# Scores of the first attention as one float32r product over stacked high and low parts

## The reference

```
Bx  = einsum('bni,bri->bnr', x, B[adapter_ids])          # rank 16
c   = einsum('bnr,bor->bno', Bx, A[adapter_ids])         # 8 samples x 128 x 512
qkv = einsum('sbh,ph->sbp', c, weight_qkv)               # 8 groups of 4 query heads, one key, one value head
attention runs over the 8 samples s, t (causal, t <= s), separately for each of the 128 rows
x   = x + (softmax(q k^T / sqrt(128)) v) @ weight_proj^T
```

## Time and profile before

| | us |
|---|---|
| median of 3 runs | 1568.53 |
| lowest and highest | 1563.63, 1569.09 |
| the profiled execution | 1554.2 |
| its span | 1552.5 |
| PE busy | 1509.9 (97%) |
| DVE busy | 1180.2 (76%) |
| ACT busy | 893.2 (58%) |
| POOL busy | 879.2 (57%) |

### The profile page before, as it was taken

How to read it: one execution, slowest core, us unless ns; L and a number is a source line. 1 busy time by engine, 2 the same in 40 slices (tenths; PEclk the granted TensorE clock), 3 DMA queues, 4 the chain that set the end, 5 groups by cost and what they waited for, 6 DMA issues and landing times.

```text
span 1552.5 us, 27376 instructions
## 1 busy us (share of the span) xinstructions
PE 1509.9 (97%) x8984; PEld 1293.2 (83%) x8984; DVE 1180.2 (76%) x2668; ACT 893.2 (58%) x2308; POOL 879.2 (57%) x1231
## 2 busy tenths in 40 slices
PE   6899999989999999999999999999999999999997
PEld 4788888778888888888888888888888888888885
DVE  3666665767888888888888878888887888777865
ACT  2433333356666666666666666666666666666641
POOL 1111234236667666766676676667666766676521
PEclk8999999999999999999999999999999999999999
DMA  6654555322222222222222222222222222311102
GB/s 209 209 161 134 148 165 162 77 82 70 69 71 73 69 71 61 76 70 70 64 72 71 71 66 70 70 71 72 70 72 66 70 69 65 89 59 48 42 27 82
DMA packets 74085, 133.39 MB, mean 86 GB/s; under 512 B 17426, under 2 KB 27026, under 8 KB 73946
## 3 DMA queue, kind: packets, MB, share of 16 engines
q1 hardware_dynamic: 56482, 97.56, 21.2%
q0 software_dynamic: 16464, 33.85, 7.5%
q10 hardware_dynamic: 1000, 0.23, 0.1%
HBM read 107.47 MB, written 7.34 MB: 74 GB/s over the span
## 4 chain that ended last, share of the span: by engine, by line
PE 91%; DVE 3%; ACT 2%; issue 2%; POOL 1%; DMA 1%; ACTq 0%; POOLq 0%; DVEq 0%; SPq 0%
PE ps_t L948 15%; PE ps_o L739 11%; PE ps_o L741 10%; PE ps_o L740 10%; PE ps_b L739 5%; PE ps_b L741 5%; PE ps_b L740 5%; PE ps_q L741 4%; PE ps_q L740 4%; PE ps_q L739 4%; PE ps_t L762 3%; PE ps_a L739 3%; PE ps_a L793 3%; PE ps_a L741 3%; PE ps_a L740 3%
## 5 line engine op out<-in xcount | busy, mean ns | idle before, releaser
L1443 ACT ACTIVATE sm<-sm,mn 128x640 f32<-128x640 f32 x256 | 211.4, 826 | 234.5 <-DVE mn L1912 234.5
L1788 DVE TENSOR_TENSOR pT_lo<-ps_t,pT_hi 128x512 fp32r<-128x512 f32 x320 | 220.2, 688 | 113.5 <-ACT pT_hi L1366 113.3
L622 POOL DMA_INDIRECT kraw<-in_L_cond_k_cache_dram,idx_a x200 | 197.5, 988 | 89.1 <-issue 74.3
L1366 ACT ACTIVATE pT_hi<-ps_t 128x512 fp32r<-128x512 f32 x320 | 188.5, 589 | 84.7 <-PE ps_t L948 84.7
L622 POOL DMA_INDIRECT vraw<-in_L_cond_v_cache_dram,idx_a x200 | 198.7, 994 | 59.6 <-issue 59.3
L948 PE MATMUL ps_t<-ident,sm 128*128 128x128 f32 x1280 | 195.7, 275 | 3.2 <-ACT sm L1453 1.5
L948 PEld LDWEIGHTS ps_t<-ident,sm 128*128 128x128 f32 x1280 | 147.9, 140 | 51.4 <-DVE qT_lo L1788 17.9
L639 POOL TENSOR_TENSOR z<-pairs_p,zl 128x128 f32<-128x128 f32 x160 | 57.9, 402 | 206.8 <-DVE pairs_p L1652 206.8
L739 PE MATMUL ps_o<-pT_lo,v_hi 128*128 128x512 f32 x320 | 129.8, 406 | 0.0
L741 PE MATMUL ps_o<-pT_hi,v_hi 128*128 128x512 f32 x320 | 125.5, 392 | 0.0
L740 PE MATMUL ps_o<-pT_hi,v_lo 128*128 128x512 f32 x320 | 124.9, 390 | 0.0
(11 more groups left out here) (257 smaller groups left out, 4370.1 us busy)
## 6 DMA issues: line engine op xcount, KB each, us to landing
fv<-st SPq DMA_DIRECT2D x128, 128.0 KB, 2.3
tab<-tab_scratch SPq DMA_DIRECT2D x64, 256.0 KB
wraw<-n_L_attn_weight_qkv_dram SPq DMA_DIRECT2D x8, 1536.0 KB, 7.3
wpraw<-_L_attn_weight_proj_dram SPq DMA_DIRECT2D x8, 1024.0 KB, 9.4
mask<-mask_scratch SPq DMA_DIRECT2D x64, 128.0 KB
wtile<-in_L_cond_Wq_dram SPq DMA_DIRECT2D x28, 256.0 KB
wtile<-in_L_cond_Wo_dram SPq DMA_DIRECT2D x28, 256.0 KB
kraw<-in_L_cond_k_cache_dram,idx_a POOLq DMA_INDIRECT x200, 2.6
```

Source lines behind the costliest of these rows:

```text
L622: pool.indirect_dma_start(raw[:, par, c, :], None, rows_d, bass.IndirectOffsetOnAxis(idx[:, k:k + 1].bitcast(U32), 0)).then_inc(arrived[pa ...
L1366: act.activation(dst, src, ACT.Copy).then_inc(t_hi, 1)
L1443: act.activation(sm[:, h, :], sm[:, h, :], ACT.Exp, bias=mn[:, h:h + 1], scale=-1.0, accum_out=den[:, h:h + 1]).then_inc(e_done, 1)
L1788: dve.tensor_tensor(lo, src, hi.bitcast(F32), ALU.subtract).then_inc(t_lo, 1)
```

## The change

For scores_s, the high and low parts are put side by side along the contraction instead of being three products. `zlT[:, 2p:2p+2, :]` is nonzero only in the 32 rows of quarter p (two samples of 16 ranks). So three quarters' rows of one product are enough for the three terms:

- `zl3`: for the pair of samples p, the high part stands in the rows of quarter p and again in quarter p + 1, the low part in quarter p + 2 (all modulo 4). `zl_rows` (ACT, 8 copies) and `zl_low` (DVE, 4 subtractions) fill it, once.
- `mix3`: four tiles, one for each pair p, of 4 heads by 32 (p + 1) columns. Quarter p holds the high part of `mix`, quarter p + 1 the low part, quarter p + 2 the high part again. In each group `mix_copy` (ACT) makes 4 copies of 32 rows by 128, 256, 384 and 512 columns, `mix_second` (ACT) 4 copies of the same sizes, and `mix_low` (DVE) 4 subtractions of the same sizes. `mix_low` waits for all four of `mix_copy`.
- `scores_s` is one float32r product of the same width on these. Product 0 waits for the first `mix_second` and `mix_low`, product 1 for all four `mix_low`.
- POOL clears `mix3` (1280 columns) and `zl3` (1024 columns) ahead of `halfs` and `mask`.
- `wT` has three slots instead of six; `zlT` lies elsewhere.
- PE does `mix_product` ahead of `z_out(1)` (in group 0: ahead of `p_group(1)`).

```diff
-        mix = at("mix", [P, HG, P], F32, 52)
-        wT = at("wT", [P, 6, NC_, P], F32, 136)
-        zlT = at("zlT", [P, N, P], F32, 168)
+        wT = at("wT", [P, 3, NC_, P], F32, 136)
+        mix3 = at("mix3", [P, 10 * P], F32R, 142)
+        zl3 = at("zl3", [P, N, P], F32R, 168)
+        zlT = at("zlT", [P, N, P], F32, 56)
...
+        def mix_tile(p):
+            first = P * (p * (p + 1) // 2)
+            return mix3[:, first:first + P * (p + 1)].rearrange("q (h m) -> q h m", h=HG)
+        def rows(q):
+            return slice(32 * (q % 4), 32 * (q % 4) + 32)
...
+            pool.memset(mix3[:].bitcast(F32), 0.0).then_inc(zl3_ok, 1)
+            pool.memset(zl3[:].bitcast(F32), 0.0).then_inc(zl3_ok, 1)
             pool.memset(halfs[:], -0.5).then_inc(iota_ok, 1)
...
             def scores_s(g, s):
+                if s % 2 == 0:
+                    pe.wait_ge(mix_two, 4 * g + s // 2 + 1)
+                    pe.wait_ge(mix_lo, 4 * g + s // 2 + 1)
+                if s == 1:
+                    pe.wait_ge(mix_lo, 4 * g + 4)
                 if s <= 1:
-                    pe.wait_ge(mix_done, g + 1)
...
-                pe.matmul(o.rearrange("p (h m) -> p h m", h=HG), zlT[:, s, :], mix[:, :, 0:R * (s + 1)],
+                pe.matmul(o.rearrange("p (h m) -> p h m", h=HG), zl3[:, s, :], mix_tile(s // 2)[:, :, 0:R * (s + 1)],
...
             def mix_copy(g):
                 act.wait_ge(mix_full, g + 1)
-                act.activation(mix[:, :, :].rearrange("p h m -> p (h m)"), s_bank(9 * g)[:, :], ACT.Copy
-                               ).then_inc(mix_done, 1)
+                if g == 0:
+                    act.wait_ge(zl3_ok, 2)
+                src = s_bank(9 * g)[:, :].rearrange("q (h m) -> q h m", h=HG)
+                for p in range(4):
+                    act.activation(mix_tile(p)[rows(p), :, :], src[rows(p), :, 0:32 * (p + 1)], ACT.Copy
+                                   ).then_inc(mix_hi, 1)
+            def mix_second(g):
+                for p in range(4):
+                    act.wait_ge(mix_hi, 4 * g + p + 1)
+                    act.activation(mix_tile(p)[rows(p + 2), :, :], mix_tile(p)[rows(p), :, :].bitcast(F32), ACT.Copy
+                                   ).then_inc(mix_two, 1)
+            def zl_rows():
+                act.wait_ge(zT_done, 2)
+                act.wait_ge(zl3_ok, 2)
+                for p in range(4):
+                    act.activation(zl3[rows(p), 2 * p:2 * p + 2, :], zlT[rows(p), 2 * p:2 * p + 2, :], ACT.Copy
+                                   ).then_inc(zl3_hi, 1)
+                for p in range(4):
+                    act.activation(zl3[rows(p + 1), 2 * p:2 * p + 2, :], zlT[rows(p), 2 * p:2 * p + 2, :], ACT.Copy
+                                   ).then_inc(zl3_two, 1)
...
+            def mix_low(g):
+                dve.wait_ge(mix_hi, 4 * g + 4)
+                src = s_bank(9 * g)[:, :].rearrange("q (h m) -> q h m", h=HG)
+                for p in range(4):
+                    dve.tensor_tensor(mix_tile(p)[rows(p + 1), :, :], src[rows(p), :, 0:32 * (p + 1)],
+                                      mix_tile(p)[rows(p), :, :].bitcast(F32), ALU.subtract).then_inc(mix_lo, 1)
```

More of the change, by code:

```diff
@@ L1317, in _ @@
                 w_copy(0, t)
+            zl_rows()
             fold_copy(0)
             p_copy(0, 0)
+            mix_copy(0)
             p_copy(0, 1)
-            mix_copy(0)
+            mix_second(0)
             p_copy(0, 2)
@@ L1336, in _ @@
                 mix_copy(i)
+                mix_second(i)
                 p_copy(i, 1)
@@ L1627, in sums_s, with zl_low @@
                                   AX.X, ALU.add).then_inc(y_red, 1)
+            def mix_low(g):
[4 more added lines that the diff above has]
+                                      mix_tile(p)[rows(p), :, :].bitcast(F32), ALU.subtract).then_inc(mix_lo, 1)
+            def zl_low():
+                for p in range(4):
+                    dve.wait_ge(zl3_hi, p + 1)
+                    dve.tensor_tensor(zl3[rows(p + 2), 2 * p:2 * p + 2, :], zlT[rows(p), 2 * p:2 * p + 2, :],
+                                      zl3[rows(p), 2 * p:2 * p + 2, :].bitcast(F32), ALU.subtract).then_inc(zl3_lo, 1)
             def soft_rows():
@@ L1694, in x2_low @@
                                   x2T_hi[:, :, s, :].bitcast(F32), ALU.subtract).then_inc(x2t_lo, 1)
+            zl_low()
             fold_low(0)
             p_low(0, 0)
+            mix_low(0)
             p_low(0, 1)
@@ L1728, in _ @@
                 x2_sum(i, 0)
+                mix_low(i)
                 x2_sum(i, 1)
```

18 lines of the change are left out of this document (13 added, 5 removed).

## The result

The changed kernel takes 1581.11 us (median of 4 runs, 1579.00 to 1582.01), the kernel before 1568.81 beside it: a ratio of 1.0088, interval 1.0060 to 1.0115. (One of the four runs of the kernel before took 2129.24 us; the ratio compares the fast runs and leaves it out.) I had forecast 1564.0 us, a little faster, with a range of 1553.5 to 1571.5; it is 0.9% slower, outside the range and on the other side.

What follows compares the result with a forecast made beforehand. PE was taken to bound groups 1 to 7, DVE the start and group 0. The terms 1.6 + 2.9 - 9.0 = -4.5 us, applied to the 1568.5 median, gave 1564.0 us, range 1553.5 to 1571.5.

Steps and rivals of the forecast that it cites:

- The start: Before the first fold: POOL's clears make DVE begin 1.6 us late, with no gap to recover it; +1.6 us.
- Gain on PE: Groups 1 to 7: the eight scores products fall from 4.03 to 1.28 us, saving PE 2.75 us a group.
- Rival 5: Scores products: float32r costs as much as native, so 1.24 us is lost in each group; 1581.7 us, chance 0.02.
- rival 1: Groups 1 to 7: no wait, PE runs on and all 2.75 us a group are saved; 1553.7 us, chance 0.15.
- The chain: ACT copies, then DVE subtractions behind the mix product: scores product 2 starts 1.24 us late, net 1.28 us saved a group.
- rival 2: Narrow operations pay in full, ACT 1.74 and DVE 1.95 us, chain 0.7 longer in eight groups; 1570.6 us, chance 0.09.
- my own sign for it: In the profile after, four mix copies on ACT over more than 1.8 us would show narrow operations costing more.
- its terms 3.5, 1.0 and 1.5: Uncertainties in us: chain (0.5 a group), group 0, and where PE's clock comes back; own range 1559.5 to 1568.5.
- Group 0: DVE bounds it; ACT's eight zl3 copies and the chain delay the first products_s from 44.75 to 47.6; +2.9 us.
- rival 4: The clock falls in every group through new waits of about 0.7 us, 2.9 lost each; 1584.3 us, chance 0.04.
- No second wait follows: Groups 1 to 7, behind product 2: PE waits no more, as DVE has 12 us of slack a group.
- Nothing behind the first stage changes: After the first stage: no term, so the second stage adds nothing to the sum.

Runs made afterwards that it cites:

- e1_before_again: The kernel before, unchanged, profiled once more on the first job's chip: 1563.86 us.
- e2_after_again: The changed kernel, unchanged, profiled once more on the first job's chip: 1580.4 us.
- e6_split: Changed kernel, but ACT first copies the whole mix product to SBUF and each scores product waits for its own tile alone: 1560.94 us, ratio 0.9967.
- e7_narrow: The kernel before plus series of ACT copies and DVE subtractions at the idle start, on all rows, 32 rows or changing quarters; no whole time given.
- e4_gathers_late: The changed kernel with POOL's 16 gathers of groups 3 to 6 moved behind the last z product of group 7: 1579.93 us, ratio 1.0112.
- f1_after_third: The changed kernel, unchanged, timed a third time, on a fourth chip: 1573.11 us, ratio 1.0072.
- job 3: Follow-up runs on a third chip, with gathers of both stages moved in the kernel before and a further changed one; the kernel before took 1554.1 us there.
- the first job: Follow-up runs on one chip: both kernels unchanged, and the changed kernel with clears or gathers moved; the kernel before took 1564.0 us there.

## Why the prediction was wrong

The steps, with the two first stages of one chip (`e1_before_again`, `e2_after_again`; in all 299.5 and 313.4, +13.9; I had -4.5). With the second stage the difference on that chip is 16.5 us, against 12.3 between the medians of the first measurement:

| stretch | before | after | change | predicted |
|---|---|---|---|---|
| to the first fold | 33.09 | 34.03 | +0.9 | +1.6 |
| group 0 | 24.25 | 29.97 | +5.7 | +2.9 |
| group 1 | 36.69 | 36.63 | -0.1 | -1.3 |
| groups 2 and 3, each | 34.06 | 33.82 | -0.2 | -1.3 |
| groups 4 to 7 in all | 137.34 | 145.17 | +7.8 | -5.1 |

The first stage misses the forecast by 18.4 us. Two steps failed. The narrow operations were priced too low: 0.95 us in each of seven groups, 6.7 in all, and 2.2 of the 2.8 us by which group 0 missed. And the sum had nothing for late starts of ACT and a falling clock, which make 9.1 us more in groups 4 to 7. The start missed by -0.7, groups 1 to 3 by another 0.5.

**Gain on PE: right, a little large.** By distances the eight products cost 1.3 us, as forecast; product 2, to which I had added 0.09 that no row showed, took 0.20 (the second product behind it starts at 151.47: 151.47 - 151.04 - 0.23). PE's busy time in a group went down by 2.3 us, and with the waits gone a group takes 31.92 us, 2.1 less than before, with 0.3 of idle time in it; I had 2.75, and where the rest went isn't worked out. Rival 5 is out, and rival 1 is what `e6_split` built.

**The chain: the price of the narrow operations was wrong.** This is the first step that failed: "between them by columns: 0.15, 0.26, 0.38, 0.49", and 0.20, 0.33, 0.47, 0.61 on DVE. I took these from operations that follow one another on the same rows, and each of the new ones works on another quarter than the one before. The two doubts that I wrote down behind it, 32 rows instead of 128 and a write to another quarter, turned out to cost nothing in `e7_narrow`; the change of rows I hadn't thought of. ACT's chain ran 0.40 longer and DVE's 0.47, 0.87 of the 0.95 us by which product 2 was later than forecast. It is rival 2's price, to which I gave 0.09: 1.74 and 1.95 there, 1.79 and 2.08 measured, so my own sign for it, copies of more than 1.8 us, was just missed. (The section of the Trainium skill that the prediction cites, "VectorE: DVE Perf Modes", "The TRN2 errata", has the latency paid by each small tile; the series of `e7_narrow` agree only where the rows change, and at 0.31 for a duration of 0.40 not where they stay.) With 0.33 instead of 1.28 saved in a quiet group the sum would have been +2.2, hardly to be told from no change; with the same price in group 0 (0.9 us on the chain, 1.3 in the copies for `zl3`) +4.4, just past the upper end of the range. (The forecast's own range is also odd: its terms 3.5, 1.0 and 1.5 don't make the 4.5 us either way that it has, and nothing says how they were put together.)

**Group 0: right in kind, half in size.** 5.7 us and not 2.9. The eight copies for `zl3` made the folded copy 2.0 us late and not 0.7 (3.4 us in the hole of 1.36, where I had 2.1), and the chain is 0.9 longer as in the other groups. The rest is the sentence that ACT "has done `p_copy(1)`, `mix_second` and `p_copy(2)` by 46.95": it had by 50.7, and `p_low(2)` stood before the first `products_s`.

**The start: right in cause**, 1.86 on DVE for 1.6, of which the clock gave 0.9 back before the first fold (the products of `z` took 8.35 us instead of 9.20, since they began later and the clock came back at about the same time). What I had not seen is that the clears could not simply be moved.

**Late starts and the clock: the second step that failed, and half of rival 4.** The sum says "No second wait follows" and has no term for the clock in groups 2 to 7; I priced a fall in every group at 0.04 because the known fall came with 3.86 us of idle. In the changed kernel the clock does not fall at the 2.2 us of idle in groups 2 and 3. It falls in groups 4 to 7, where the held mix copy adds up to 1.6 us to the same gap; in group 4 the granted clock is 0.56 and 0.58 on the mean between 186 and 190 us, right behind the three waits. PE's waits are 1.40 and 0.63 us in group 3, and 1.30, 1.45 and 0.63 in group 4. Without the hold (`e4_gathers_late`), or with 0.2 us of it (`f1_after_third`), one group of these four has a fall (clock 0.95) and three with nearly the same waits (1.40 and 1.45 in front of product 1, 0.63 in front of product 2) have none, so they are at the edge; without the waits (`e6_split`) the clock is 1.00 in all of groups 2 to 7. A fall cost 1.4 us (35.17 in group 4 of `e4_gathers_late`, 33.76 in group 5), half of my 2.9.

**"Nothing behind the first stage changes": the code doesn't, the time does**, by 2.7 us on that chip (waits for `kvown` 8.8 and 12.5 us). These waits presumably depend on the phase between POOL's gathers and ACT's copies; that is argued, not shown. Why other lines ahead of the second stage change how many of the steps are held was not tried.

**The profile I read** shows nothing held, like those of job 3, and is 14 us under the median. On which chip it was taken isn't on record. I noted the 14.3 us and applied the sum to the median as if they were spread evenly. They were not: on the chip of the first job 1.8 us more lay in held mix copies and 8.9 in the second stage, and the change adds to the first of these just where PE had no more slack.

## What to carry to other kernels

A chain of small operations that PE waits for is priced by what the rows do: operations in a row on the same rows overlap, a change of rows cost 0.1 us each time on ACT and DVE (at 256 columns), and the wait should be for the one tile that is needed next, with the PSUM bank freed by one wide copy first. A gain on the bounding engine that was reckoned at 2.75 us a group was worth 0.2 while the product that it speeds up had to wait 2 us, and three quarters of it once it needn't. And where the profiled execution is faster than the timed ones by more than the effect one looks for, ask first which waits the others have that this one lacks.

## What was not expected of the hardware

- ACT's start is held while POOL issues gathers, by 0.2 to 1.6 us. The mix copies that are held by more than 0.3 us start at one of two distances behind a gather's start (1.84 to 1.94, 1.14 to 1.21). It isn't equal in all jobs: in the kernel before, the same copies are 0.9 to 1.0 us late on the first two chips and on time on the third, with 1564, 1566 and 1554 us for the kernel. What is shared between the two engines isn't known.
- DVE's conversion of 8 columns took 1.91 us instead of 0.17 while POOL cleared SBUF.
- ACT's copies of 256 columns on the same rows follow each other at 0.31 us, on changing quarters at 0.43, at a duration of 0.40 to 0.42 both times.
